# Reordering one stage of a two-layer kernel: offset products ahead of matrix products, value products last, last two gathers undivided

## The reference, cut to what matters

```
def step(S, inp):
    q_t, k_t, v_t, g_t, b_t = inp
    S = S * jnp.exp(g_t)[..., None, None]
    mem = jnp.einsum('bhk,bhkv->bhv', k_t, S)
    delta = (v_t - mem) * b_t[..., None]
    S = S + jnp.einsum('bhk,bhv->bhkv', k_t, delta)
    o_t = jnp.einsum('bhk,bhkv->bhv', q_t, S)
    return (S, o_t)
```

## Time and profile before

| what | value |
|---|---|
| median of 3 runs | 886.2 us (884.87, 886.2, 888.82) |
| profiled execution | 885.32 us |
| its span | 883.2 us |
| busy: PE, DVE, ACT, POOL | 787.4, 542.7, 252.3, 210.1 us |
| mean granted TensorE clock | 0.949 of full |

### The profile page before, as it was taken

The page is one execution under the profiler, slowest core; times in us unless marked ns, Lnnn a source line. Parts: engine busy times, 40 slices in busy tenths (PEclk is TensorE's granted clock), DMA queues, the critical chain, the costliest instruction groups (busy, mean ns, idle before and its releaser), DMA issues.

```text
span 883.2 us, 11650 instructions
## 1 busy us (share of the span) xinstructions
PE 787.4 (89%) x4040; PEld 566.3 (64%) x4040; DVE 542.7 (61%) x1302; ACT 252.3 (29%) x402; POOL 210.1 (24%) x191
## 2 busy tenths in 40 slices
PE   5889999888999999998988499799885999999974
PEld 4322333576777777776446478578652899999963
DVE  4599993654444444446799998995478244333426
ACT  2456667332333343333540001221310100000000
POOL 3550000021222222220031000474001344444310
PEclk9989999987999999999999699899997999999995
DMA  9683000101111111140221003400011899999944
GB/s 297 167 195 74 2 3 5 51 19 36 36 53 36 53 36 53 36 144 1 84 96 36 0 1 92 122 1 1 1 48 34 319 340 342 336 350 344 341 138 155
DMA packets 38034, 98.85 MB, mean 112 GB/s; under 512 B 5262, under 2 KB 18118, under 8 KB 37030
## 3 DMA queue, kind: packets, MB, share of 16 engines
q1 hardware_dynamic: 33894, 87.91, 31.1%
q0 software_dynamic: 3648, 9.97, 3.1%
q10 hardware_dynamic: 448, 0.39, 0.2%
HBM read 85.35 MB, written 13.69 MB: 112 GB/s over the span
## 4 chain that ended last, share of the span: by engine, by line
PE 63%; DVE 28%; DMA 4%; ACT 2%; issue 2%; SPq 1%; POOL 0%; ACTq 0%; DVEq 0%; POOLq 0%
PE psum L1246 16%; PE psum L1513 9%; PE psum L1523 8%; PE psum L1257 7%; PE psum L1146 3%; DVE arena L2003 3%; PE psum L1135 3%; PE psum L1125 3%; DVE arena L2062 3%; DVE arena L2055 2%; DVE small L1674 2%; DVE arena L1915 2%; PE psum L1407 1%; PE psum L1325 1%; PE psum L1264 1%
## 5 line engine op out<-in xcount | busy, mean ns | idle before, releaser
L1246 PE MATMUL psum<-xr,wr 128*128 128x512 f32 x600 | 158.8, 415 | 1.1 <-DVE arena L1823 1.1
L1246 PEld LDWEIGHTS psum<-xr,wr 128*128 128x128 f32 x600 | 115.9, 194 | 25.4 <-issue 1.3
L666 POOL TENSOR_TENSOR wr<-ring,wr 128x512 fp32r<-128x512 f32 (+1 forms) x50 | 54.3, 1104 | 197.8 <-ACT wr L829 197.8
L1674 DVE TENSOR_REDUCE small<-psum 128x1 f32<-128x512 f32 x128 | 80.9, 684 | 9.2 <-PE psum L1125 8.5
L1513 PEld LDWEIGHTS psum<-arena 128*128 128x128 f32 x700 | 83.4, 191 | 3.4 <-issue 1.5
L1513 PE MATMUL psum<-arena 128*128 128x128 f32 x700 | 83.9, 274 | 1.1 <-ACT arena L1013 1.1
L1523 PE MATMUL psum<-arena 128*128 128x256 f32 x350 | 81.8, 379 | 1.9 <-DVE arena L2227 1.9
L2216 DVE TENSOR_SCALAR arena<-psum,arena 128x256 f32<-128x256 f32 x35 | 16.9, 484 | 101.4 <-PE psum L1523 101.4
L1786 DVE TENSOR_TENSOR hid<-hid,psum 128x512 f32<-128x512 f32 x50 | 34.4, 688 | 68.4 <-ACT hid L835 68.4
L1257 PE MATMUL psum<-hr,wr 128*128 128x512 f32 x300 | 76.1, 389 | 0.2 <-DVE hr L1761 0.2
L808 ACT ACTIVATE arena<-psum 128x1024 f32<-128x1024 f32 x64 | 63.0, 1023 | 27.1 <-PE psum L1135 26.3
(11 more groups left out here) (360 smaller groups left out, 1232.2 us busy)
## 6 DMA issues: line engine op xcount, KB each, us to landing
arena<-in_w1u SPq DMA_DIRECT2D x35, 642.5 KB
arena<-in_w1d SPq DMA_DIRECT2D x35, 640.0 KB
ring<-in_w SPq DMA_DIRECT2D x25, 384.0 KB, 3.0
part_scratch<-arena SPq DMA_DIRECT2D x12, 256.0 KB, 4.2
arena<-z_scratch SPq DMA_DIRECT2D x8, 384.0 KB, 6.5
arena<-part_scratch SPq DMA_DIRECT2D x9, 256.0 KB, 7.8
qkv_scratch<-arena SPq DMA_DIRECT2D x4, 512.0 KB, 2.8
arena<-qkv_scratch SPq DMA_DIRECT2D x4, 512.0 KB, 4.0
```

Of the source, the lines that this page charges most:

```text
L666: pool.tensor_tensor(wr0[:, k, LO, part], ring0[:, k, part], wr0[:, k, HI, part], ALU.subtract).then_inc(s["w0_lo"], 1)
L1246: ins = pe.matmul(bank[2 * b + m][:, :], wr0[:, k, w, lo:lo + P], xr[:, x, f, half(b)], start=(f == 0 and (w, x) == PARTS[0]), stop=(f == ...
L1674: dve.tensor_reduce(nm[:, g % 2, at16:at16 + 1], full("scores", n), AX, ALU.max, negate=True).then_inc(s["bank_free"], 1)
```

## The change

DVE's order becomes: eight query products; offset products of k = 0, 1, 2 (2048 elements each, three tiles `nprod`); a loop over k with the matrix product (1024 elements, two tiles `mprod`), and between the adds of the M tree the offset product of k + 3, which waits for `n_sum` of at least k + 3 (the query sums now count as the first two); the diagonal; a wait for all ten sums; all eight value products; the scan. PE's order becomes: query sums, offset sums, a wait for `m_done` and all eight `n_in`, the two spreads, all output sums, the units; gathers 0 and 1 stay where they are, gathers 2 and 3 follow unit 8, each whole. ACT copies Q' before the offsets. SP writes Q' out first, reads back two of its four chunks, then does the offsets without waiting for `m_done`, then the two other chunks; POOL waits for two chunks at its start and for the others at unit 4. Tiles are laid out anew to match. The block of query sums that PE loses behind the spreads is the one that it gains in front of the offset sums; it is shown once.

```
-        mn = [t.rearrange("p (j x c) -> p j x c", j=C, x=XR)
-              for t in (arena[:, 0:XR * CT], arena[:, XR * CT:2 * XR * CT], KPROD[:, 0:XR * CT])]
+        nprod = [arena[:, n * DV * CT:(n + 1) * DV * CT].rearrange("p (j x c) -> p j x c", j=C, x=DV)
+                 for n in range(3)]
+        mprod = [arena[:, 3 * DV * CT + n * DK * CT:3 * DV * CT + (n + 1) * DK * CT]
+                 .rearrange("p (j x c) -> p j x c", j=C, x=DK) for n in range(2)]
+        assert 3 * DV * CT + 2 * DK * CT <= end
...
-        Nscan = arena[:, 21 * DV * CC:21 * DV * CC + DV * CT]
-        assert 21 * DV * CC + DV * CT <= end
+        Nscan = KPROD[:, 2304:2304 + DV * CT]
...
-            lo = {0: KPROD[:, 4352:], 1: arena[:, end + 1536:], 2: arena[:, 7424:], 3: v2[:, DV * CT // 2:],
-                  4: KPROD[:, XR * CT:], 5: arena[:, end:], 6: arena[:, 2048:], 7: arena[:, 0:]}[i]
-            x = lo[:, 0:DV * CC * (i + 1)]
+            n = DV * CC * (i + 1)
+            if i == C - 1:
+                x = arena[:, end + 4 * CT * DK + 2 * CT:][:, 0:n]
+            else:
+                x = arena[:, DV * CC * i * (i + 1) // 2:][:, 0:n]
...
+            def queries_out(pair, name):
+                for g in pair:
+                    for v in range(VG):
+                        sp.dma_start(qB[g][v * 32:(v + 1) * 32].rearrange("p k n -> p (k n)"),
+                                     q_dram.rearrange("(h g) x -> g h x", g=NCG)[g]).then_inc(s[name], 16)
...
+            sp.wait_ge(s["qp_in"], 2)
+            sp.dma_start(q_dram, Qp).then_inc(s["to_dram"], 16)
+            sp.wait_ge(s["to_dram"], 16 * 6)
+            queries_out((0, 1), "qB_first")
...
-            sp.wait_ge(s["m_done"], 1)
...
-            sp.wait_ge(s["to_dram"], 16 * 6)
+            sp.wait_ge(s["to_dram"], 16 * 7)
...
-            sp.wait_ge(s["qp_in"], 2)
-            sp.dma_start(q_dram, Qp).then_inc(s["to_dram"], 16)
-            sp.wait_ge(s["to_dram"], 16 * 7)
-            for g in range(NCG):
-                for v in range(VG):
-                    sp.dma_start(qB[g][v * 32:(v + 1) * 32].rearrange("p k n -> p (k n)"),
-                                 q_dram.rearrange("(h g) x -> g h x", g=NCG)[g])\
-                      .then_inc(s["qB_rest" if g else "qB_first"], 16)
+            queries_out((2, 3), "qB_rest")
...
-            pool.wait_ge(s["qB_first"], 16 * VG)
+            pool.wait_ge(s["qB_first"], 16 * VG * 2)
...
-                if n0 == CC:
-                    pool.wait_ge(s["qB_rest"], 16 * VG * (NCG - 1))
+                if n0 == 2 * CC:
+                    pool.wait_ge(s["qB_rest"], 16 * VG * 2)
...
-            for k in range(DK):
-                act.wait_ge(s["n_sum"], k // 2 * 2 + 2)
-                act.activation(Nsb.rearrange("p (g c v k) -> p k g v c", g=VG, c=CC, v=VV)[:, k],
-                               n_bank(k).rearrange("p (g v c) -> p g v c", g=VG, v=VV), ACT.Copy).then_inc(s["n_in"], 1)
...
-                act.wait_ge(s["n_sum"], DK + x + 1)
+                act.wait_ge(s["n_sum"], x + 1)
...
+            for k in range(DK):
+                act.wait_ge(s["n_sum"], 2 + k // 2 * 2 + 2)
+                act.activation(Nsb.rearrange("p (g c v k) -> p k g v c", g=VG, c=CC, v=VV)[:, k],
+                               n_bank(k).rearrange("p (g v c) -> p g v c", g=VG, v=VV), ACT.Copy).then_inc(s["n_in"], 1)
...
-                    pe.wait_ge(s["x_prod"], O_ORDER.index(t) + 1 + (0 if t < 6 else 2 * DK))
+                    pe.wait_ge(s["x_prod"], 2 * DK + O_ORDER.index(t) + 1)
...
-            o_sums(O_ORDER[:6])
+            pe.wait_ge(s["decays"], 3)
+            for t in range(C):
+                pe.wait_ge(s["x_prod"], t + 1)
+                to = bank[4 + t // 4][:, t % 4 * CT:(t % 4 + 1) * CT]
+                pe.matmul(to, ident[:, :], qa[:, t * CT:(t + 1) * CT], start=True, stop=False, skip_group_check=True)
+                for j in range(t + 1):
+                    ins = pe.matmul(to, ident[:, :], q_prod(t)[:, j].rearrange("p x c -> p (x c)"), start=False,
+                                    stop=(j == t), skip_group_check=True)
+                if t % 4 == 3:
+                    ins.then_inc(s["n_sum"], 1)
...
-                pe.wait_ge(s["x_prod"], 6 + k + 1)
+                pe.wait_ge(s["x_prod"], C + k + 1)
+                if k == 4:
+                    pe.wait_ge(s["qp_in"], 2)
...
-                    ins = pe.matmul(n_bank(k), ident[:, :],
-                                    mn[k % 3][:, j, 0:DV, :].rearrange("p x c -> p (x c)"),
+                    ins = pe.matmul(n_bank(k), ident[:, :], nprod[k % 3][:, j].rearrange("p x c -> p (x c)"),
...
-                    pe.wait_ge(s["n_in"], 2)
+                    pe.wait_ge(s["n_in"], DK)
...
-            pe.wait_ge(s["qp_in"], 2)
...
-            def gather(g, lo, hi):
+            o_sums(O_ORDER)
...
+            def gather(g):
...
-                            bank[n].rearrange("p (t v c) -> p t v c", t=2, v=DV)[:, :, v * VV:(v + 1) * VV, lo:hi],
-                            selgv[:, g, v, :], seqU[:, g, 2 * n:2 * n + 2, :, lo:hi],
-                            start=False, stop=(g == NCG - 1 and hi == CC), skip_group_check=True)
-                    if g == NCG - 1 and hi == CC:
+                            bank[n].rearrange("p (t v c) -> p t v c", t=2, v=DV)[:, :, v * VV:(v + 1) * VV, :],
+                            selgv[:, g, v, :], seqU[:, g, 2 * n:2 * n + 2].rearrange("p t v c -> p (t v c)"),
+                            start=False, stop=(g == NCG - 1), skip_group_check=True)
+                    if g == NCG - 1:
...
-                if u in (2, 4, 6):
+                if u in (2, 4):
...
-                    gather(u // 2 - 1, 0, CC)
-                if u == 7:
-                    pe.wait_ge(s["state_out"], 7)
-                    gather(NCG - 1, 0, 8)
+                    gather(u // 2 - 1)
+            gather(2)
...
-            gather(NCG - 1, 8, CC)
+            gather(3)
...
-            o_products(O_ORDER[:6])
...
-            M3 = Msb.rearrange("p (c k x) -> p k x c", c=CC, k=DK)
...
-            def matrix_part(k, lo, hi):
-                return mn[k % 3][:, lo:hi, DV:XR, :]
...
-            def product(k, lo, hi):
-                return dve.tensor_tensor(mn[k % 3][:, lo:hi], Xt[:, lo:hi],
-                                         Ru[:, C + k, lo:hi].unsqueeze(2).broadcast_to((P, hi - lo, XR, CC)), ALU.mult)
...
-            def second_sum(k):
-                ch.need(summed)
-                return ch.mark(dve.tensor_tensor(matrix_part(k, 0, 2), matrix_part(k, 0, 2), matrix_part(k, 2, 4), ALU.add))
...
-            def third_sum(k):
-                ch.need(summed)
-                return ch.mark(dve.tensor_tensor(M3[:, k], mn[k % 3][:, 0, DV:XR, :], mn[k % 3][:, 1, DV:XR, :], ALU.add))
...
-            for k in range(DK):
-                if k >= 3:
-                    dve.wait_ge(s["n_sum"], k - 2)
-                product(k, 0, 4)
-                if k:
-                    summed = second_sum(k - 1)
-                product(k, 4, C).then_inc(s["x_prod"], 1)
-                if k:
-                    summed = third_sum(k - 1)
-                dve.wait_ge(s["x_prod"], 6 + k + 1)
-                summed = ch.mark(dve.tensor_tensor(matrix_part(k, 0, 4), matrix_part(k, 0, 4), matrix_part(k, 4, C),
-                                                   ALU.add))
-            summed = second_sum(DK - 1)
-            summed = third_sum(DK - 1)
-            ch.need(summed)
-            diag = Msb.rearrange("p (c e) -> p c e", c=CC)[:, :, 0:DK * DK:DK + 1]
-            dve.tensor_tensor(diag, diag, by_step(A0)[:, C - 1, :].unsqueeze(2)
-                              .broadcast_to((P, CC, DK)), ALU.add).then_inc(s["m_done"], 1)
...
-            dve.wait_ge(s["n_sum"], 6)
...
-            dve.wait_ge(s["n_sum"], DK)
-            o_products(O_ORDER[6:])
...
+            M3 = Msb.rearrange("p (c k x) -> p k x c", c=CC, k=DK)
...
+            def product(to, k, lo, hi):
+                return dve.tensor_tensor(to, Xt[:, :, lo:hi, :],
+                                         Ru[:, C + k].unsqueeze(2).broadcast_to((P, C, hi - lo, CC)), ALU.mult)
...
+            def offset_product(k):
+                if k >= 3:
+                    dve.wait_ge(s["n_sum"], k)
+                product(nprod[k % 3], k, 0, DV).then_inc(s["x_prod"], 1)
...
+            def pair_sum(to, x, n):
+                return ch.mark(dve.tensor_tensor(to, x[:, 0:n], x[:, n:2 * n], ALU.add))
...
+            def last_sum(k):
+                return ch.mark(dve.tensor_tensor(M3[:, k], mprod[k % 2][:, 0], mprod[k % 2][:, 1], ALU.add))
...
+            for k in range(3):
+                offset_product(k)
+            for k in range(DK):
+                x = mprod[k % 2]
+                if k >= 2:
+                    ch.need(ended)
+                formed = ch.mark(product(x, k, DV, XR))
+                if k:
+                    ch.need(summed)
```

(20 more changed lines are left out.)

## The result

Nine runs of each: 882.33 us (877.82 to 883.29) against 889.15 before (884.87 to 891.93), ratio 0.9916, 95% interval 0.9891 to 0.9941. The changed kernel is 6.8 us faster by the medians; 5.8 had been forecast, with a median of 880.4. Its profiled execution took 881.27 us with a span of 879.1.

What follows compares the result with a forecast made beforehand. Before the scan DVE's work with one stall was taken to bound the kernel, and PE the stage's end. Gains of 1.7 + 4.1 = 5.8 us bring the median from 886.2 to 880.4; range 877.2 to 883.4.

Steps and rivals of the forecast that it cites:

- The start of the scan: Part 1: DVE's new order brings the scan's first reduce to 552.7 against 554.41, 1.7 us gained.
- The one stall: Before its fourth offset product DVE waits for PE's offset sum 0, from 509.7 to 512.8: 3.1 us.
- The cover: The offsets' way through DRAM to the slot is ready at 550.7, two us before the scan's first reduce.
- the trip: The offsets' way to DRAM and back before the scan, taken as 11.7 us.
- Rival (a): Clock rises sooner, DVE's stall is small, the offsets' trip decides the scan's start: gain 3.7, total 7.8, 878.4; chance 0.13.
- The end of the stage: Part 2, from unit 6's sum to the last gather: 10.9 against 15.0 us, 4.1 gained.
- The forecast split: Of the gain at the stage's end, 3.6 us from the undivided gather and half a us from waits.
- Rival (d): At the stage's end the undivided gather saves nothing, matmuls cost by columns: total 2.2, 884.0; chance 0.02.
- (b): DVE's stall takes the whole gain before the scan (4.8 us or more), only part 2 stays: 882.1; chance 0.15.
- (c): Clock rises only well into the offset sums, DVE stands 13.9 us: 5 us slower, 891.2; chance 0.04.
- Everything behind the last gather moves with it: Code after the stage waits on the last gather's copies alone, so it shifts with the gather.

Runs made afterwards that it cites:

- e12: The changed kernel with the gathers of the kernel before (the order alone), run a second time; ratio 1.0000 to the kernel before.
- e3: The changed kernel with the gathers of the kernel before (the order alone), first run; ratio 1.0005 to the kernel before.
- e5: The changed kernel with 14 more idle-time matmuls on PE between query sums and offset sums; 886.67 us, a single execution.
- e6: The changed kernel with 62 idle-time matmuls in PE's pause before the query sums, DVE's order untouched; 881.74 us against 889.65, ratio 0.9895.
- e7: The changed kernel with each offset product from k = 3 on two turns later in DVE's loop; 884.42 us against 889.65, ratio 0.9945.
- e9: The changed kernel with gather 2 back behind unit 6 and gather 3 whole; 877.94 us, a single execution.
- e2: The kernel before with gathers 2 and 3 whole and behind unit 8; 885.21 us against 887.75, ratio 0.9962.
- e10: The changed kernel with 64 idle-time matmuls before the query sums, offset products one turn later, gathers 0 and 1 behind the next spread; 878.3 us against 888.48, ratio 0.9876.
- e4: The changed kernel with 54 idle-time matmuls before the query sums and offset products from k = 3 one turn later; 876.71 us against 887.75, ratio 0.9871.
- e8: The changed kernel with SP's wait for m_done put back in front of the write of the offsets; 883.78 us, one execution.

## Why the prediction was right, and where it was not

The mechanism came about as told: one stall of DVE behind offset sum 0, no other wait before the scan, and a tail that lost the price of one gather. The closeness of the median is in part luck. Forecast was 880.4 from a level of 886.2, the median of three runs; over nine the kernel before has 889.15. The level was 3.0 us too low and the gain 1.0 too small, and 882.33 lies 1.9 above the forecast because the two work against each other.

- **The start of the scan.** Forecast gain 1.7, measured 1.7 (1.7 to 1.8 over the three profiles). The one stall was forecast at 3.1 and was 3.1 to 3.25 (3.3 to 3.4 in e12 and e3); e5 shows that DVE queues behind it one for one, e6 that 2.4 of it is the half clock. Product times by the slope from two rows (2.2 and 1.14 us) came out as 2.20 and 1.13.
- **The cover.** Forecast margin of the slot 2 us, measured 0.8. The term that was mis-sized is the trip: 11.7 from the rows of before, 13.3 to 13.8 in the changed kernel. It did not decide, but e7 shows how close it stands.
- **Rival (a).** It did not come about, for the clock rose no sooner. e6 makes its condition: the offset sums then end sooner as well (write issued at 39.2 us of the stretch against 41.6), the trip was 11.7, and A gained 4.1 where the rival had 3.7. Its price was sound, but 0.7 us of it was lost in S.
- **The end of the stage.** Forecast 4.1, measured 3.9 in every profile. Unit 8's sum took 2.05 instead of 1.85. The forecast split, 3.6 and 0.5, was 3.5 and 0.4 (e9). Whole gathers of 128 columns cost 3.58 us each, halves of 64 columns 3.5 to 3.8, and e2 shows the gain of an undivided gather on its own. Rival (d) falls. The rule of the Trainium skill that I set against it ("TensorE: Matmul & The Clock Gate", "Back-to-back issue gap") is the section's formula for the isolated gap; for a stream of weight loads and matmuls, which a gather is, the same section says that both set the spacing and that the formula counts too little for few columns. The rows agree with that part (0.110 us an instruction at 64 columns, 0.112 at 128), and the prediction had left it out.
- **Rivals (b) and (c).** The clock rose 5.1 us into the query sums and not later, and no other wait was added. Neither came about.
- **What the sum lacked.** "Everything behind the last gather moves with it" was wrong by 1.5 us: D. The step looked at waits alone, not at the clock under the code behind the stage. By it, the total is 7.0 and not 5.8. The measured 6.8, 5.5 and 8.0 us surround both, and all three intervals hold both, so D is shown by the profiles and not by the medians. In e3 and e12 the same term takes 1.0 of the 1.4 to 1.6 us that A gained.

What stays open: what places the clock's fall in D. Where a kernel was profiled again it followed the kernel, not the execution, but e5 and e10 share the changed kernel's 65.5, and e4, e6, e7, e8 and e9, with the same code behind the stage, have 66.8 to 67.0. Equal sums hide different places: e2, e6 and e8 have slow logits (4.9 us), while e4 and e9 have fast ones (3.8 to 3.9) and lose 1.4 us behind them, where the clock is at half once more for some 7 us instead of 3.5. I found nothing in these profiles that would have told it ahead.

## What to carry to other kernels

A piece that is moved ahead on one engine moves work ahead on the engine that consumes it, and a queue that restarts cold sets the price: cost the consumer at the clock it will have, and then fill its pause with idle-time matmuls. Where two paths end within a us or two of each other, taking a stall off the one shows the other (e7); what shortens both pays, alone (e6, where the clock brings the offset sums forward too) or with the stall's move (e4, e10). Small gains are read by stretches of the trace, which here repeat to 0.2 us, and not by medians, which here scatter by several; but the stretches behind the change belong in the sum as well.

## What the runs showed of the hardware that I had not expected

The same write of 1024 KB to DRAM took two times, by kernel: from its issue to that of the reads behind it 5.2 to 6.1 us in the changed kernel (three profiles), e3, e5, e7, e9 and e12, and 3.85 to 3.9 us before and in e2, e4, e6, e8 and e10. The windows of the changed kernel show a rate above 400 GB/s for about 2.5 us and then a last us at 25, with the reads issued at 546.58:

```profile
542.00:543.00 1.00, 0.00 (x0) 0.00 (x0) 1.00 (x2) 0.00 (x0) 0.00 (x0) 0.79 1.08 426
543.00:544.00 1.00, 0.00 (x0) 0.00 (x0) 0.93 (x4) 0.00 (x0) 0.00 (x0) 0.50 1.01 410
544.00:545.00 1.00, 0.00 (x0) 0.00 (x0) 0.93 (x3) 0.00 (x0) 0.00 (x0) 0.50 0.50 205
545.00:546.00 1.00, 0.72 (x1) 0.50 (x2) 1.00 (x3) 0.00 (x0) 0.00 (x0) 0.50 0.06 25
```

Why that tail comes with some kernels and not with others is open. PE's state during the write does not decide it: in e7 PE was busy at full clock and the write was long, in e6 PE was idle and it was short, in e8 PE was busy at half clock and it was short. The tail cost nothing in the changed kernel, and in e7 it is about 2 of the 4.23 us that DVE waits.

Matmuls of 64 columns with fresh weights each ran at 0.110 us an instruction (32 in 3.52 us), the pace of those of 128 columns (32 in 3.57 us).
